# Loading three input groups in two transfers each, of unequal numbers of partitions

## The reference, cut to what matters

```python
def reference(x, cond_8, L0_cond_weight, L0_cond_mask, L0_cond_bias):
    # x (32, 256, 256), cond_8 (32, 8), weight (8, 256, 256), mask (256, 256), bias (256,), all float32
    masked_w = L0_cond_weight * L0_cond_mask[None, :, :]
    w_bot = jnp.einsum('bg,got->bot', cond_8, masked_w)
    return x + jnp.einsum('bnt,bot->bno', x, w_bot) + L0_cond_bias
```

## Time and profile before

| what | us |
|---|---|
| median of 3 runs | 67.26 |
| lowest, highest | 67.02, 67.57 |
| profiled execution | 66.99 |
| its span, first to last instruction | 65.2 |

### The profile page before, as it was taken

The page is one execution under the profiler, slowest core; times in us unless marked ns, Lnnn a source line. Parts: engine busy times, 40 slices in busy tenths (PEclk is TensorE's granted clock), DMA queues, the critical chain, the costliest instruction groups (busy, mean ns, idle before and its releaser), DMA issues.

```text
span 65.2 us, 1490 instructions
## 1 busy us (share of the span) xinstructions
PE 59.5 (91%) x645; PEld 54.9 (84%) x645; DVE 47.5 (73%) x34; ACT 47.9 (73%) x40; POOL 6.0 (9%) x15
## 2 busy tenths in 40 slices
PE   2999399999999999999999999999999999999900
PEld 1268297779888899999999999999999999999900
DVE  2108939977948989999999999979999992340200
ACT  2500869696979999999999799999779986006420
POOL 5500862350000000000000000000000000000000
PEclk9999999999999999999999999999999999999999
DMA  0899999999999139935799999999999239917492
GB/s 0 249 413 368 407 368 319 373 430 431 412 422 402 50 45 377 402 151 236 216 271 249 405 442 427 402 420 445 395 417 417 93 143 407 397 50 299 178 370 95
DMA packets 5589, 20.20 MB, mean 310 GB/s; under 512 B 592, under 2 KB 1104, under 8 KB 4688
## 3 DMA queue, kind: packets, MB, share of 16 engines
q1 hardware_dynamic: 5296, 19.89, 79.4%
q10 hardware_dynamic: 288, 0.23, 1.2%
HBM read 11.73 MB, written 8.39 MB: 309 GB/s over the span
## 4 chain that ended last, share of the span: by engine, by line
PE 81%; DMA 6%; ACT 5%; issue 1%; DVE 1%; SPq 1%
PE slots L398 20%; PE slots L397 20%; PE slots L396 20%; PE slots L411 11%; PE slots L296 8%; DMA x_ring<-in_masked 6%; ACT w_raw L484 5%; PE slots L290 2%; ACT weights L514 1%; DVE weights L530 1%; SPq L204 1%
## 5 line engine op out<-in xcount | busy, mean ns | idle before, releaser
L396 PE MATMUL slots<-x_hi,w_hi 128*128 128x256 f32 x112 | 31.4, 280 | 0.0
L398 PE MATMUL slots<-x_hi,w_lo 128*128 128x256 f32 x112 | 31.2, 279 | 0.0
L397 PE MATMUL slots<-x_lo,w_hi 128*128 128x256 f32 x112 | 31.2, 279 | 0.0
L397 PEld LDWEIGHTS slots<-x_lo,w_hi 128*128 128x128 f32 x112 | 21.1, 188 | 0.0
L396 PEld LDWEIGHTS slots<-x_hi,w_hi 128*128 128x128 f32 x112 | 21.1, 188 | 0.0
L398 PEld LDWEIGHTS slots<-x_hi,w_lo 128*128 128x128 f32 x112 | 21.1, 188 | 0.0
L536 DVE TENSOR_TENSOR x_lo<-x_ring,x_hi 128x2048 fp32r<-128x2048 f32 (+1 forms) x8 | 16.1, 2020 | 1.7 <-ACT x_hi L450 1.7
L450 ACT CAST x_hi<-x_ring 128x2048 fp32r<-128x2048 f32 (+1 forms) x8 | 13.5, 1696 | 1.5 <-DMA x_ring<-in_x 1.2
L468 ACT ACTIVATE weights<-slots,smalls 128x1024 f32<-128x1024 f32 x10 | 10.9, 1121 | 4.8 <-PE slots L398 4.8
L545 DVE TENSOR_TENSOR w_lo<-w_raw,w_hi 128x2048 fp32r<-128x2048 f32 x6 | 13.7, 2285 | 0.2 <-ACT w_hi L456 0.2
L484 ACT COPY w_raw<-slots 128x1024 f32<-128x1024 f32 x8 | 8.0, 1013 | 6.2 <-PE slots L296 6.0
(11 more groups left out here) (22 smaller groups left out, 15.4 us busy)
## 6 DMA issues: line engine op xcount, KB each, us to landing
out<-weights SPq DMA_DIRECT2D x15, 512.0 KB, 4.4
x_ring<-in_x SPq DMA_DIRECT2D x7, 1024.0 KB, 9.6
x_ring<-in_masked SPq DMA_DIRECT2D x4, 512.0 KB, 5.3
weights<-in_weight SPq DMA_DIRECT2D x4, 256.0 KB, 5.5
x_ring<-in_x SPq DMA_DIRECT2D x2, 512.0 KB, 8.6
out<-weights SPq DMA_DIRECT2D x1, 256.0 KB, 2.4
out<-weights SPq DMA_DIRECT2D x1, 128.0 KB, 2.4
out<-weights ACTq DMA_DIRECT2D x1, 128.0 KB, 2.2
```

Source lines behind the costliest of these rows:

```text
L396: nc.tensor.matmul(dst, wh, xh, start=(k == 0), stop=False)
L397: nc.tensor.matmul(dst, wh, xl, start=False, stop=False)
L398: last = nc.tensor.matmul(dst, wl, xh, start=False, stop=(k == KC - 1))
```

## The change

Groups 1, 2 and 3 are loaded in two transfers each: the first 120, 104 or 88 partitions, then the remaining 8, 24 or 40. Group 0 and groups 4 to 7 are loaded as before. The wait in `high_x` counts 32 for the first use of slots 1 to 3, and 16 more for each later one.

```diff
+FIRST_ROWS = (P, 120, 104, 88)
@@ block.sync
             def load_group(g):
-                sp.dma_start(x_ring[:, g % XS, :], x[g]).then_inc(x_loaded[g % XS], 16)
+                rows = FIRST_ROWS[g] if g < XS else P
+                sp.dma_start(x_ring[0:rows, g % XS, :], x[g, 0:rows]).then_inc(x_loaded[g % XS], 16)
+                if rows < P:
+                    sp.dma_start(x_ring[rows:P, g % XS, :], x[g, rows:P]).then_inc(x_loaded[g % XS], 16)
@@ block.scalar, high_x
-                act.wait_ge(x_loaded[g % XS], 16 * (g // XS + 1))
+                act.wait_ge(x_loaded[g % XS], 16 * (g // XS + (2 if g % XS else 1)))
```

## The result

The changed kernel took 74.48 us, median of 4 runs (74.23 to 74.67), the kernel before 67.14 us, median of 4 (66.81 to 67.57). The ratio is 1.108, with a 95% interval from 1.102 to 1.114. The prediction was 67.1 us, within 66.6 to 67.7, with 0.06 for slower. It was wrong. Executions over 1.5% above the fastest of the same kernel, one of the ten of experiment 1 and two of the four of experiment 9, are left out of comparisons.

The account below looks back on a forecast made before the run. TensorE, busy 91% and never waiting from 17.38 us on, was taken as the bound. With 0 on SP, ACT and landings the profiled 66.99 us stayed; half of the runs' 0.27 us above it gave 67.1 us, range 66.6 to 67.7.

Parts of the forecast that it names:

- the price of a row: Loads of groups 1 to 3: each 8 KB row costs a DMA engine 0.31 us.
- (b): Split loads: 15, 13 and 11 engines carry the first parts; the most loaded has 9, 19 and 31 rows; costs nothing.
- Rival D: Split loads: only 8 engines carry each part, 5.0 us a group, 70.5 us in total; chance 0.03.
- lag: End of the loads: one or two straggling DMA engines hold the landing back by some 2 us.
- TensorE without waits and an early load worth nothing: From 17.38 us to the end TensorE doesn't wait, so an earlier load of groups 1 to 3 can't shorten the execution.
- The cover of 0.29 us at group 1: ACT's `x_hi(1)`, at 18.70 us: only a delay of more than 0.29 us delays TensorE, by the excess.
- The cover of about 0.5 us behind group 3: After group 3's user: 0.23 us before `x_lo(4)` begins and another 0.31 us in that chain absorb delay.
- Issues and wait free: Three more load issues on SP and a higher count in ACT's `high_x` wait cost 0.
- Group 4 covered by 3.7 us: Group 4's load lands at 27.7 us, its user begins at 31.35: 3.7 us margin against at most 2.2 us leftover.
- First and small parts on 15 and 8, 13 and 12, 11 and 10 engines: DMA engines carrying the two parts of groups 1, 2 and 3, by the Trainium skill's rule on dividing rows.
- Rate of an engine unchanged: Split loads: each DMA engine still takes 0.31 us a row, as with whole transfers of 128 rows.
- the margins of 2.2 us at groups 2 and 3: Loads of groups 2 and 3 land at 21.1 and 23.5 us, 2.2 us before their users at 23.35 and 25.73.

Follow-up runs that it names:

- experiment 1: Kernel before, with groups 1 to 3 loaded in two transfers each, cut by columns with all 128 partitions in both: 67.13 us against 67.21 before.
- experiment 9: Kernel before, with groups 1 to 3 loading only the first 4 KB of each row: 66.78, 68.97, 66.73 and 67.86 us against 67.18 before.
- experiment 11: Changed kernel, with groups 1 to 3 split into 96 and 32 partitions each: 72.61 us.
- experiment 7: Changed kernel, with only group 1 split, into 120 and 8 partitions, and groups 2 and 3 whole: 71.41 us.
- experiment 10: Changed kernel, with only group 3 split, into 88 and 40 partitions, and groups 1 and 2 whole: 68.86 us.

## Why the prediction was wrong

**The step that failed** is the price of a row. The prediction said "Eight rows of 8 KB an engine in 2.45 us make 0.31 us a row" and used this for every dealing of the rows. It measured 0.57 us a row, and 188 GB/s where there were 410. The spread (b) itself was right, down to the number of engines. But the bounds only asked how many rows an engine gets, not what a row costs when the engines write elsewhere. Rival D, 8 engines at the full price of a row, came nearest, for the wrong reason; its 70.5 us were too few as well. With the measured 0.57, the same sum gives group 3 at 14.2 + 31 × 0.57 = 31.9 without lag and 33.9 with 2 us of it, around the measured 33.3 (from which the price was read in part), and group 1 at 16.2 − 2 + 9 × 0.57 = 19.3 to 21.3, short of the measured 22.8. So one price for all rows isn't quite enough: it ran from 0.31 to 0.62 us a packet with the partitions written, and the last count can come further behind the bulk where packets are slow (experiment 11).

**Point by point.** TensorE without waits and an early load worth nothing: right for the profiled execution, shown by experiment 9. The cover of 0.29 us at group 1: experiment 7 agrees, 4.3 us for 4.5 us late. The cover of about 0.5 us behind group 3: right, experiment 10. Issues and wait free: right, experiment 1. Group 4 covered by 3.7 us: it cost nothing, but by luck. It was issued at 23.58 and landed 12.7 us later, at 36.3, 8.6 us after the forecast 27.7 and well past the 31.35 at which it was needed before; only its user was itself 7.6 us late, at 38.95. First and small parts on 15 and 8, 13 and 12, 11 and 10 engines: right. Rate of an engine unchanged: wrong, and it decides everything. The rule of the Trainium skill ("DMA: Bandwidth & Descriptors", "Rules for kernel authors") that two transfers to disjoint halves of the partitions serialize was weighed as neutral. Halves show that such a pair can lose four tenths of the rate (229 GB/s against the 393 of even and odd).

**The range** rested on the margins of 2.2 us at groups 2 and 3. They were enough for an uneven load and not for half the rate, and nothing in the profile of before told the two apart, for all of its large transfers have 128 partitions. Such a cost should have been bounded by the rate itself. At half the rate three groups take 14.7 us, group 3 lands at 14.2 + 14.7 + 2 = 30.9, 5.2 us after 25.73, and with 0.5 us of cover the loss is 4.7 us: a bound like this would have made the range reach 72 us, most of the way to 74.48.

**What stays open.** Which engine takes which partition was not seen. The model's consecutive rows fit 120, 104, 88, 112, 126, 96 and 60, but neither 128 nor the 64 even ones, which must be dealt otherwise. So leaving 128 partitions seems to change the dealing itself, and that is argued from the model alone. That 8 ports are what each half reaches is the account of the Trainium skill ("SBUF — State Buffer", "Door 1: The DMA port swizzle"); the runs show that the choice of destination partitions alone takes the rate from 423 to 215 or 226 GB/s (15 to 20 us). Which engines come last, and why, is not known.

## What to carry to other kernels

Load 128 partitions at a time, and if a transfer must be cut, cut it along the row. By columns it cost nothing. By partitions it cost 1.3 to 7.3 us, except for the 64 even and 64 odd ones, which cost nothing either. A DMA share near 1 with half of the GB/s meant here that each packet took twice as long, not that there was more to move. When a change alters the shape of a transfer, bound its rate as well as its load.

## What the runs showed of the hardware that was not expected

Two transfers of 64 partitions ran at 393 GB/s as even and odd ones and at 229 GB/s as halves. Transfers of 120 and 8, 104 and 24, 88 and 40 partitions ran on 15, 8, 13, 12, 11 and 10 engines and together at 188 GB/s, while 126 and 2, on 14 and 2 engines, reached 320 (all from 20 to 21 us). Fewer engines with more rows each were the quicker ones, and a packet of 8 KB took 0.31 to 0.62 us depending on the partitions written.
